# Row maxima of attention taken in query order, without their transpose

## What is computed

```python
q = (x @ Wq.T + bq).reshape(Bb, Nn, H, hd).transpose(0, 2, 1, 3)
...
a1 = jax.nn.softmax(jnp.einsum('bhnd,bhmd->bhnm', q1, k1) * scale, axis=-1)
x1 = jnp.einsum('bhnm,bhmd->bhnd', a1, v1).transpose(0, 2, 1, 3).reshape(Bb, Nn, C // 2)
```

## Time and profile before

| | |
|---|---|
| median of 3 runs | 5091.62 us (5087.88 to 5100.66) |
| the profiled execution | 5054.9 us |
| its span, first to last instruction | 5052.8 us |
| attention, first to last reduction of line 1665 | 2474.5 to 4954.0 us |
| mean granted TensorE clock | 0.968 of full speed |

### The profile page before, as it was taken

The page is one execution under the profiler, slowest core; times in us unless marked ns, Lnnn a source line. Parts: engine busy times, 40 slices in busy tenths (PEclk is TensorE's granted clock), DMA queues, the critical chain, the costliest instruction groups (busy, mean ns, idle before and its releaser), DMA issues. The chain is left out here.

```text
span 5052.8 us, 90487 instructions
## 1 busy us (share of the span) xinstructions
PE 4497.4 (89%) x32649; PEld 2022.6 (40%) x32649; DVE 4091.9 (81%) x4841; ACT 3546.8 (70%) x6195; POOL 1709.0 (34%) x1147
## 2 busy tenths in 40 slices
PE   6778778778775899999899998999998999999998
PEld 3225225225223788888522222222222222222225
DVE  5997997998896332222499998999998999999996
ACT  5765766776672111121499998999998999999993
POOL 1982993893894222222111111120011311121003
PEclk8998998999998999999999999999999999999998
DMA  2403502102103555555211112111112211222116
GB/s 81 158 1 109 192 1 92 43 1 69 49 1 100 194 188 194 183 200 190 69 35 34 40 36 51 39 48 37 36 34 51 56 37 35 52 54 69 22 29 188
DMA packets 333694, 390.71 MB, mean 77 GB/s; under 512 B 172019, under 2 KB 288590, under 8 KB 322446
## 3 DMA queue, kind: packets, MB, share of 16 engines
q0 software_dynamic: 42784, 208.59, 12.7%
q1 hardware_dynamic: 286174, 174.18, 12.7%
q10 hardware_dynamic: 4352, 2.66, 0.2%
HBM read 248.78 MB, written 137.57 MB: 76 GB/s over the span
## 5 line engine op out<-in xcount | busy, mean ns | idle before, releaser
L1665 DVE TENSOR_REDUCE at_mpart<-at_ps 128x1 f32<-128x1024 f32 x2048 | 2348.7, 1211 | 95.1 <-PE at_ps L1554 63.0
L1650 ACT ACTIVATE at_E<-at_ps 128x512 f32<-128x512 f32 x4096 | 2222.3, 594 | 167.3 <-PE at_ps L1569 81.8
L1576 PE MATMUL at_ps<-at_E,at_vst 128*32 128x256 f32 x16400 | 1315.1, 392 | 25.0 <-ACT at_osb L1631 21.6
L1554 PE MATMUL at_ps<-at_ks,at_qs 48*128 48x512 f16 x4096 | 801.4, 388 | 54.3 <-DMA at_qs<-at_mrow 28.4
L1569 PE MATMUL at_ps<-at_qs,at_ks 50*128 50x512 f16 x4096 | 791.0, 383 | 21.5 <-ACT at_E L1650 21.0
L1438 POOL DMA_INDIRECT at_y<-yd,at_gidx x128 | 129.4, 1011 | 1670.0 <-DVE at_mx L1670 1586.6
L890 POOL TENSOR_TENSOR l_work<-l_work 128x1024 f32<-128x1024 f32 x252 | 593.8, 2356 | 34.0 <-issue 0.4
L1362 ACT ACTIVATE at_late<-at_ps 128x256 f32<-128x256 f32 x288 | 110.6, 384 | 638.6 <-PE at_ps L1305 638.6
L1576 PEld LDWEIGHTS at_ps<-at_E,at_vst 128*32 128x32 f32 x16400 | 326.6, 108 | 565.7 <-issue 411.9
L1554 PEld LDWEIGHTS at_ps<-at_ks,at_qs 48*128 48x128 f16 x4096 | 196.4, 92 | 875.2 <-DVE at_mpart L1665 449.0
L786 PE MATMUL l_ps<-l_bc,l_sel 96*128 96x512 bf16 x1024 | 319.4, 397 | 247.0 <-DVE l_work L924 124.1
(11 more groups left out here) (263 smaller groups left out, 4196.4 us busy)
## 6 DMA issues: line engine op xcount, KB each, us to landing
xd<-l_zero SPq DMA_DIRECT2D x4, 5120.0 KB, 32.9
yd<-l_zero SPq DMA_DIRECT2D x4, 5120.0 KB, 33.5
at_qs<-qp SPq DMA_DIRECT2D x132, 128.0 KB
at_ks<-kp SPq DMA_DIRECT2D x396, 32.0 KB
ot<-at_osb SPq DMA_DIRECT2D x516, 17.0 KB
at_qs<-qp SPq DMA_DIRECT2D x132, 64.0 KB
at_vst<-vp SPq DMA_DIRECT2D x65, 128.0 KB, 4.7
at_qs<-at_mrow SPq DMA_DIRECT2D x516, 2.0 KB
```

Of the source, the lines that this page charges most:

```text
L1554: mm = pe.matmul(ring[n % 2][:, r, :], m.qs[row, buf, bass.ts(i, P)], m.ks[row, buf, bass.ts(kh, BANK)], start=True, stop=True)
L1576: mm = pe.matmul(O[32 * q:32 * q + 32, :], m.vst[:, par, SLOTS_A * kk + sl, :], m.E[:, sl % 4, kk, bass.ts(q, QG)], start=(sl == 0 and kk ...
L1650: act.activation(m.E[:, sl % 4, kk, bass.ts(hf, BANK)], S[chunk(sl, 2 * hf + kk) % 3], ACT.Exp, scale=scale).then_inc(s.ex, 1)
L1665: dve.tensor_reduce(m.mpart[:, job:job + 1], ring[n % 2].rearrange("p a b -> p (a b)"), AX_X, ALU.max).then_inc(s.ring_free, 1)
```

## The change

- A `peak` product takes every eighth query (p x 8 + i) in place of 128 neighbours, so that `mx` of 128 x 8 is in query order as it lies: partition p holds queries 8p to 8p + 7. The weights are read out of `m.qs` with a step of 8 elements (16 bytes).
- The transpose on PE and its bank of `S` go; a step has 32 chunks in place of 33 and the three banks turn on from step to step. `mneg` goes. ACT makes the high part from `mx` at once (128 x 8), at the end of slot 1 in place of slot 2. DVE makes the low part from `mx` with one scalar_tensor_tensor (128 x 8) after slot 3 in place of slot 4.
- `rows` is the same code, but its source `mrow` is now 128 partitions of 16 bytes: each of the four DMAs is made of 128 pieces of 16 bytes in place of 8 of 256.
- `mpart` has two halves that take turns. `last` moves behind the first reduction of the next step, and no reduction waits for it. It waits for the low row of the step before instead (`mlo`). `mfin` starts one lower: a count that POOL waits for is reached behind the first reduction of a step, where it was reached at the end of the step before.
- The copy of O moves ahead of the fourth exponential of slot 0 (it was behind it).
- In `run_experts`, the first 32 reductions have the same form, with one transpose and its waits gone; the second set of maxima is left for step 0 of `attend`.

```diff
+def peak_queries(m, row, buf, i):
+
+    half = slice(i // 8 * QB, (i // 8 + 1) * QB)
+    return m.qs[row, buf, half].rearrange("r (p i) -> r i p", i=8)[:, i % 8, :]
...
-    TURN_AT, LOW_AT = 2, 4
-    TURN_CHUNK = 4 * TURN_AT + 2
-    CHUNKS = 4 * SLOTS_A + 1
-
-    def chunk(sl, c):
-
-        l = 4 * sl + c
-        return l + 1 if l >= TURN_CHUNK else l
+    HIGH_AT, LOW_AT, COPY_AT = 1, 3, (0, 1, 1)
+    CHUNKS = 4 * SLOTS_A
+
+    def score_bank(t, l):
+
+        return S[(CHUNKS * t + l) % 3]
 
     def drained(t, l):
 
@@ -1551,22 +1546,16 @@
                 pe.wait_ge(s.ring_free, wait)
                 for r in range(2):
                     row = slice(64 * r, 64 * r + STACK)
-                    mm = pe.matmul(ring[n % 2][:, r, :], m.qs[row, buf, bass.ts(i, P)], m.ks[row, buf, bass.ts(kh, BANK)], start=True, stop=True)
+                    mm = pe.matmul(ring[n % 2][:, r, :], peak_queries(m, row, buf, i), m.ks[row, buf, bass.ts(kh, BANK)], start=True, stop=True)
                 mm.then_inc(s.ring, 1)
-            def turn(t):
-
-                pe.wait_ge(s.mfin, t + 2)
-                pe.wait_ge(s.ex, drained(t, TURN_CHUNK - 3))
-                pe.transpose(S[TURN_CHUNK % 3][0:8, 0:P], m.mx[:], m.ident[:]).then_inc(s.turned, 1)
-
...
-                        if sl == TURN_AT and hf == 0:
-                            turn(t)
...
-            def turn(t):
-
-                act.wait_ge(s.turned, t + 2)
-                act.wait_ge(s.mlo, t + 1)
-                act.activation(m.mneg[:], S[TURN_CHUNK % 3][0:8, 0:P], ACT.Identity, scale=-(2.0 ** -ROW_EXP)).then_inc(s.ex, 1)
-                act.wait_ge(s.ex, drained(t, TURN_CHUNK))
+            def high_row(t):
+
+                act.wait_ge(s.mfin, t + 2)
                 act.wait_ge(s.mrow, ROW * (t + 1))
-                act.copy(m.mrow[:, 0, :], m.mneg[:]).then_inc(s.mhi, 1)
+                act.activation(m.mrow[:, 0, :], m.mx[:], ACT.Copy, scale=-(2.0 ** -ROW_EXP)).then_inc(s.mhi, 1)
             def step(t, par, pairs):
                 for sl in range(SLOTS_A):
-                    if sl == 1:
-                        copy_out(t, par, pairs)
                     act.wait_ge(s.av, SLOTS_A * t + sl - 2 + AV0)
                     for hf in range(2):
                         act.wait_ge(s.score, PAIRS * t + 2 * sl + hf + 1)
                         for kk in range(2):
-                            act.activation(m.E[:, sl % 4, kk, bass.ts(hf, BANK)], S[chunk(sl, 2 * hf + kk) % 3], ACT.Exp, scale=scale).then_inc(s.ex, 1)
-                        if sl == TURN_AT and hf == 0:
-                            turn(t)
+                            if (sl, hf, kk) == COPY_AT:
+                                copy_out(t, par, pairs)
+                            act.activation(m.E[:, sl % 4, kk, bass.ts(hf, BANK)], score_bank(t, 4 * sl + 2 * hf + kk), ACT.Exp, scale=scale).then_inc(s.ex, 1)
+                    if sl == HIGH_AT:
+                        high_row(t)
...
-            def peak(job, n, ready):
+            def peak(job, half, n, ready):
                 dve.wait_ge(s.ring, ready)
-                dve.tensor_reduce(m.mpart[:, job:job + 1], ring[n % 2].rearrange("p a b -> p (a b)"), AX_X, ALU.max).then_inc(s.ring_free, 1)
-
-            def last(ready):
+                dve.tensor_reduce(m.mpart[:, half, job:job + 1], ring[n % 2].rearrange("p a b -> p (a b)"), AX_X, ALU.max).then_inc(s.ring_free, 1)
+
+            def last(half, ready):
 
                 dve.wait_ge(s.ring_free, ready + RF0)
-                dve.tensor_reduce(m.mx[:], m.mpart[:].rearrange("p (i c) -> p i c", c=2), AX_X, ALU.max).then_inc(s.mfin, 1)
+                dve.tensor_reduce(m.mx[:], m.mpart[:, half, :].rearrange("p (i c) -> p i c", c=2), AX_X, ALU.max).then_inc(s.mfin, 1)
 
             def low_row(t):
                 dve.wait_ge(s.mhi, t + 2)
-                dve.tensor_tensor(m.mrow[:, 1, :], m.mneg[:], m.mrow[:, 0, :], ALU.subtract).then_inc(s.mlo, 1)
+                dve.scalar_tensor_tensor(m.mrow[:, 1, :], m.mx[:], -(2.0 ** -ROW_EXP), m.mrow[:, 0, :], ALU.mult, ALU.subtract).then_inc(s.mlo, 1)
 
             def step(h, t, half):
                 local = 0
 
-                dve.wait_ge(s.mfin, t + 2)
+                dve.wait_ge(s.mfin, t + 1)
                 for sl in range(SLOTS_A):
                     for kh in range(2):
-                        peak(2 * sl + kh, PRO + local, PRO + NRING * t + local + 1)
+                        peak(2 * sl + kh, half, PRO + local, PRO + NRING * t + local + 1)
+                        if local == 0:
+                            dve.wait_ge(s.mlo, t + 1)
+                            last(1 - half, PRO + NRING * t)
                         local += 1
                     if sl == LOW_AT:
                         low_row(t)
-                last(PRO + NRING * t + local)
...
-            sb("mpart", [P, 16], F32, c2); sb("mx", [P, 8], F32, c2); sb("mneg", [8, P], F32, c2)
-            sb("mrow", [8, 2, P], F16, c2)
+            sb("mpart", [P, 2, 16], F32, c2); sb("mx", [P, 8], F32, c2);
+            sb("mrow", [P, 2, 8], F16, c2)
```

More of the change, by code:

```diff
@@ L1102 @@
 ROW = 64 * 1
-ATT_SEMS = "init loaded v_loaded v_free score ex av o_copy o_st0 o_st1 ring ring_free mfin turned mneg mhi mlo mrow"
+ATT_SEMS = "init loaded v_loaded v_free score ex av o_copy o_st0 o_st1 ring ring_free mfin mhi mlo mrow"
 def list_blocks(nc, io, m):
@@ L1325, in peak @@
                         pe.wait_ge(a.ring_free, job)
-                    if job == 16:
-                        pe.wait_ge(a.mneg, 1)
                     for r in range(2):
                         row = slice(64 * r, 64 * r + STACK)
-                        mm = pe.matmul(FIRST[:, r, :], m.qs[row, 0, bass.ts(i, P)], m.ks[row, 0, bass.ts(kh, BANK)], start=True, stop=True)
+                        mm = pe.matmul(FIRST[:, r, :], peak_queries(m, row, 0, i), m.ks[row, 0, bass.ts(kh, BANK)], start=True, stop=True)
                     mm.then_inc(a.ring, 1)
@@ L1365, in _ @@
                     if n == PEAK_AT + 18:
[L1366 to L1369, removed]
+                        act.wait_ge(a.mfin, 1)
+                        act.activation(m.mrow[:, 0, :], m.mx[:], ACT.Copy, scale=-(2.0 ** -ROW_EXP)).then_inc(a.mhi, 1)
             @block.vector
@@ L1375, in first_peaks @@
                     if job is not None:
[L1376 to L1377 removed]
                         dve.wait_ge(a.ring, job + 1)
[L1379 to L1380 removed]
+                        dve.tensor_reduce(m.mpart[:, job // 16, job % 16:job % 16 + 1], FIRST.rearrange("p a b -> p (a b)"), AX_X, ALU.max).then_inc(a.ring_free, 1)
+                        if job == 15:
                             dve.wait_ge(a.ring_free, job + 1)
[L1382 removed]
+                            dve.tensor_reduce(m.mx[:], m.mpart[:, 0, :].rearrange("p (i c) -> p i c", c=2), AX_X, ALU.max).then_inc(a.mfin, 1)
                     if n == PEAK_AT + 19:
                         dve.wait_ge(a.mhi, 1)
[L1385 removed]
+                        dve.scalar_tensor_tensor(m.mrow[:, 1, :], m.mx[:], -(2.0 ** -ROW_EXP), m.mrow[:, 0, :], ALU.mult, ALU.subtract).then_inc(a.mlo, 1)
                 dve.memset(m.one3, 1.0)
@@ L1568, in scores @@
                     row = slice(64 * r, 64 * r + STACK + 2)
-                    mm = pe.matmul(S[(l + r) % 3], m.ks[row, j, bass.ts(sl, P)], m.qs[row, j, half * QB + hf * BANK:half * QB + (hf + 1) * BANK],
+                    mm = pe.matmul(score_bank(t, l + r), m.ks[row, j, bass.ts(sl, P)], m.qs[row, j, half * QB + hf * BANK:half * QB + (hf + 1) * BANK],
                                    start=True, stop=True)
@@ L1616, in _ @@
             for kk in range(2):
[L1617 removed]
+                pe.wait_ge(s.ex, drained(t - 1, 4 * (SLOTS_A - 1) + 2 + kk))
                 values(SLOTS_A - 1, kk, (HEADS - 1) % 2)
```

12 lines of the change are left out of this document (4 added, 8 removed).

## The result

The changed kernel takes 5051.48 us (median of 4 runs, 5042.08 to 5055.07) against 5091.26 us before on the same chip: ratio 0.9916, 95% interval 0.9897 to 0.9935, 40 us less. Forecast were 115 us less, and 4945 to 5055 as the range: the sign is right, the size is a third of it. Run once more on another chip, where the kernel before takes 5049.94 us, it takes 5011.99, ratio 0.9923 (0.9906 to 0.9939). The profiled execution of before (5054.9 us) fits this second level and not the median of the first chip. The stages ahead of attention say the same: attention starts at 2474.5 us in the profile of before and at 2476.7 in the second profile of the changed kernel, but at 2502.0 in the first.

What follows compares the result with a forecast made beforehand. DVE's 2048 reductions at 1.13 us were taken to bound attention, with PE close behind. Border 55, low row 13, transpose and copy 15, row transfers 32 sum to 115 us: 5091.6 to 4977 us, range 4945 to 5055.

Steps and rivals of the forecast that it cites:

- the load at no cost: PE's strided weight load for `peak`: at most some 20 ns above 92 ns, taken as no cost; bounds 92 to 190.
- late rows: PE's waits for DMA out of `mrow`: rows pass in front of POOL's reads, 32 of 35 us saved; bounds 0 and 35.
- DVE's pace: Attention's reductions on DVE follow each other every 1.13 us; DVE leads PE by some 2%.
- The borders: Between steps on DVE: loss falls from 0.55 to 0.12 us at 127 borders, 55 us saved; bounds 32 and 70.
- the low row: DVE's low-part operation, now 128 x 8: 0.12 us lost in place of 0.22, 13 us saved; bounds 0 and 28.
- PE's lateness: PE late behind the copy of O and the transpose: 15 of 19 us saved; bounds 0 and 19.
- Rival 1: Strided load on PE takes 139 ns, PE leads, step 18.6 us, 32 us above the forecast: 5009 us; chance 0.13.
- The threshold of 35 ns: PE's half slot can lengthen up to about 0.035 us, as DVE's step has two small operations besides its reductions.
- with no effect at all: PE's half slot can give up 1.13 - 1.11 = 0.02 us without any effect.
- Rival 3: Row DMA pieces take turns with POOL's read pieces, so 32 us aren't saved: 5009 us, or 5030; chance 0.10.
- The copy: Copy of O one exponential earlier shrinks PE's wait; together with the transpose's removal, 15 of 19 us saved.

Runs made afterwards that it cites:

- neighbours: The changed kernel with peak products taking 128 neighbouring queries again as weights (packed load; wrong row order, score scale 2^-8 of its value): 4963.61 us, ratio 0.9827.

## Why the prediction was wrong

*The step that failed: the load at no cost.* The sum has DVE leading throughout, at 1.13 us a reduction, and the strided load in PE's half slot at nothing. The load went from 92 to 140 ns, the half slot from 1.11 to 1.157 us, and PE led: 37 us in the profile and 48 in the timed runs (`neighbours`). The further losses, below, are late rows counted as saved and long low rows that the sum doesn't have.

*DVE's pace and what can be saved: right, once the load is packed.* In `neighbours` reductions are 1.13 apart. Add up, in its trace and in that of before, what the intervals between reductions have above 1.131 us, with the few that are over 1.2 us too long left out (late rows, long low rows, ends of batches). The borders take 64 us before and 1 in `neighbours`, where `last` costs another 8; the low row 29 and 13; PE's lateness ahead of the seventh reduction of a step 21 and nothing. So 55, 15 and 21 us were saved, where the sum had 55, 13 and 15. In all, attention is 83 us shorter there than before. Add what late rows and long low rows still take, about 20 us (PE's waits for rows are 16.5 us and were to be 3, and slow half slots follow) and 28 - 6 = 22 us, and it is 125 where the sum said 115.

*The strided weights.* I put the load "at the lower end, at most some 20 ns more, since the half-precision load of 128 columns is much nearer to 92 than the fp32 ones", and so at no cost. The row of the same data type was no guide to a strided load. Rival 1 had named what came, a load of 139 ns, a step of 18.6 us (18.64 by the median) and 32 us; it was given 0.13. Its 139 was luck in part: it is the shortest load of line 1295 (the median is 141), and no run shows why a packed fp32 load and this one take the same. The threshold of 35 ns lies between the two loads that were run, 16 ns more at 4 to 15 us and 48 ns more at 37 to 48 us; nothing tests it more closely, and the 20 ns "with no effect at all" look too generous.

The Trainium skill, "SBUF — State Buffer", Door 1: The DMA port swizzle, had the rule that crossing to a new 16-byte line costs. The trace agrees in the sign, 48 ns more where every column is a line of its own. It doesn't agree with the limits that the same note gives, at least two hits in a line for full rate and a free stride of up to 8 bf16 elements: the measured load isn't free with two columns to a line (108 ns), nor with a step of 8 half-precision elements (140), and the measurement decides. The other page that I had cited, "TensorE: Matmul & The Clock Gate" of the Trainium skill, Weight-path perf modes, lets the chunks of a fast load be packed or strided but gives no time for either, so it was no argument for a load at no cost.

*Late rows: what makes them late was right, the time of their meeting wrong.* The sum had the rows pass in front of POOL's reads, 32 us saved. In step 33 SP issued them at 3138.35 and POOL its reads at 3139.76, so they did go first, by 1.4 us. But the low row had been held up for 1.5 us (1.68 in place of 0.16), and SP was at its four DMAs until 3140.88, so that the last of them met the reads. PE waits 14 us there as before; the wait of 12 us at step 68 is gone, and that at step 97 is 3 us where it was 1.6. In all PE's waits for rows fell from 28.4 to 17.4 us: 11 saved, 21 not. Rival 3 had the pieces taking turns with the reads, and the DMA records show that. Whether small pieces lose more by it than large ones isn't shown: in the kernel before, 32 pieces of 256 bytes, sent 0.85 us behind the reads, were late by as much in the same step.

*The long low rows: not in the prediction at all.* Moving an operation on DVE from 11.4 to 9.4 us into the step (by the medians) put it beside POOL's tensor_tensor operations, and these moved too, as `mfin` comes later. The low row of the kernel before, in ns:

```profile
L1674 DVE TENSOR_TENSOR at_mrow<-at_mneg,at_mrow x128: 260/268/1296, 2490.4 to 4948.2; 8x128 f16<-8x128 f32 x128
```

It was busy for 40.0 us in all, 6 us above 128 times its median: eight of them met POOL's operations already then. Line 1658 is busy for 43.6 us in the first profile and 42.4 in the second with a median of 0.156, so 24 and 22 us above it. That is some 17 us lost, and part of the late rows. The Trainium skill, "SBUF — State Buffer", Who interferes with whom, says that a DVE instruction with two SBUF inputs contends with a GpSimd instruction that reads SBUF and that the later one is blocked for the whole of the other. The trace agrees to 0.02 us (4091.91 and 4091.89), and also in that the one-input `last` and the reductions never last longer than 0.16 and 1.23 us, beside POOL's operations too. I looked up what the new operation costs alone and not whom it meets.

*The copy: right for the kernel before, not for the one without the border.* "Together I take 15 of the 19 us": alone it gives 21 to 25 us, and with the border gone 46 to 51 hang on it. What the changed kernel itself would take without this part wasn't run.

Together, in attention of the second profile: 115 - 37 (load) - 21 (late rows) - 17 (long low rows) = 40, measured 2479.5 - 2433.2 = 46. With the 48 us of the timed runs for the load it would be 29, against the 38 to 40 measured there; the account closes to some 10 us and no better. That the measured time lies inside the range of 4945 to 5055 says nothing for the sum: the range was made wide for the rivals, and two of these, 1 and in part 3, came together.

## What to carry to other kernels

When an edit changes the access pattern of an operand, price the operation by a row of that pattern. Where no row has it, the cost is open, and if the engine that it falls on has only 2% to spare behind the leader, the case in which that engine takes the lead deserves a large chance. When an operation moves in time, look at what the other engines do at its new place (shared ports, transfers in flight), and at what moves with the semaphore it signals. And two waits in one loop can hide each other: the gain of removing one is only known once the other is priced without it.

## What the runs showed of the hardware

- The weight load of 128 half-precision columns took 92 ns packed, 108 with a step of 8 bytes, 140 with one of 16 bytes, each by its median over 4096 loads; the recorded time of the matmul behind it grew along (388, 404 and 436 ns by their means).
- DVE's scalar_tensor_tensor with two inputs in SBUF, 0.156 us by its median, lasted up to 2.90 us beside POOL's tensor_tensor: all 17 long ones of the first profile end 0.02 or 0.03 us after one of these. Of the tensor_reduces none was held up (1.23 us at most).
- Rows that met reads in 8 KB pieces were late by 14 us, with 512 pieces of 16 bytes as with 32 of 256; with the reads in four parts, one a step, in 4 KB pieces and away from the rows, the wait was 0.2 us.
- The kernel before took 5091 us on one chip and 5050 to 5052 on the three of the later runs.
